# Values weighted by three products of rounded halves, and ranks copied out of PSUM by ScalarE

## The reference

```python
# attention over each sequence, on an input that the gate has scaled
scores = einsum('bqd,bkd->bqk', Q, K) * scale          # causal
attn = softmax(scores)
out = einsum('bqk,bkd->bqd', attn, V) @ Wo.T            # V @ Wo.T is one product V' here
x = x + out
# a layer per sequence (base layer plus a product of rank 8), applied to x
# then attention over the 32 sequences at each position, with 16 heads and 4 key-value heads,
# a router, and two of 8 experts for each of the 8192 rows (a dropped row beyond each expert's capacity)
```

## Time and profile before

| | |
|---|---|
| Three runs | 1309.61, 1312.0, 1320.82 us; median 1312.0 |
| Profiled execution | 1307.97 us, its span 1306.1 us |
| Mean granted TensorE clock | 0.93 of full speed |
| Busy over the span: TensorE, VectorE, ScalarE, GpSimd | 88%, 68%, 64%, 44% |
| TensorE busy, sequences 90 to 400 us | 310.0 of 310 us |
| TensorE busy, positions 429 to 765 us | 307.3 of 336 us |

### The profile page before, as it was taken

One profiled execution on the slowest core, in us unless ns is written; L12 is line 12 of the kernel. 1 busy time (PEld: TensorE's weight loads), 2 busy tenths in 40 slices (PEclk: granted clock), 3 DMA queues, 4 the chain that ended last, 5 costly groups with the idle time before them and its releaser, 6 DMA issues. The chain is left out here.

```text
span 1306.1 us, 25180 instructions
## 1 busy us (share of the span) xinstructions
PE 1151.2 (88%) x8121; PEld 1040.6 (80%) x8153; DVE 886.7 (68%) x2214; ACT 831.1 (64%) x1910; POOL 578.6 (44%) x564
## 2 busy tenths in 40 slices
PE   4499999999998898898989874489999999999985
PEld 2289999999997787787778763489989988888975
DVE  2546565656564787887887853697777778787763
ACT  1057666666665697877787652456677766676762
POOL 0012121212121243877787777246655544554455
PEclk9789999999999798988898886699999999999998
DMA  9633232333231122433343447258777768686763
GB/s 314 166 95 120 92 112 92 112 92 112 92 97 49 38 80 71 139 114 121 121 127 120 124 123 229 76 137 190 176 180 183 202 163 198 167 188 177 188 144 49
DMA packets 119517, 175.43 MB, mean 134 GB/s; under 512 B 14880, under 2 KB 89920, under 8 KB 118848
## 3 DMA queue, kind: packets, MB, share of 16 engines
q1 hardware_dynamic: 92800, 139.63, 34.7%
q0 software_dynamic: 26592, 34.24, 14.0%
HBM read 107.96 MB, written 67.69 MB: 134 GB/s over the span
## 5 line engine op out<-in xcount | busy, mean ns | idle before, releaser
L1548 POOL DMA_INDIRECT out_rows<-y,row x142 | 237.3, 1671 | 238.8 <-DVE y L1777 120.8
L1651 ACT ACTIVATE hh<-ph 128x512 fp32r<-128x512 f32 (+1 forms) x172 | 95.1, 553 | 154.4 <-issue 128.1
L1708 DVE TENSOR_TENSOR hl<-h,hh 128x512 fp32r<-128x512 f32 (+1 forms) x172 | 102.7, 600 | 94.3 <-ACT h L1652 80.4
L175 PE MATMUL py<-w2h,hh 128*128 128x256 f32 x568 | 160.7, 283 | 1.7 <-DVE y L1777 1.1
L177 PE MATMUL py<-w2h,hl 128*128 128x256 f32 x568 | 160.7, 283 | 0.0
L176 PE MATMUL py<-w2l,hh 128*128 128x256 f32 x568 | 160.7, 283 | 0.0
L175 PE MATMUL ph<-xh,w1h 128*128 128x512 f32 (+1 forms) x344 | 128.9, 375 | 34.2 <-issue 27.8
L1113 POOL DMA_INDIRECT slot_rows<-kept,slot x112 | 116.0, 1036 | 32.8 <-issue 30.8
L176 PE MATMUL ph<-xl,w1h 128*128 128x512 f32 (+1 forms) x344 | 125.4, 364 | 0.0
L177 PE MATMUL ph<-xh,w1l 128*128 128x512 f32 (+1 forms) x344 | 124.8, 363 | 0.0
L175 PEld LDWEIGHTS py<-w2h,hh 128*128 128x128 f32 x568 | 108.9, 192 | 2.9 <-issue 1.9
(11 more groups left out here) (309 smaller groups left out, 3565.0 us busy)
## 6 DMA issues: line engine op xcount, KB each, us to landing
w1e<-in_moe_w SPq DMA_DIRECT2D x43, 512.0 KB
w2e<-in_moe_w SPq DMA_DIRECT2D x43, 512.0 KB
x_rows<-x SPq DMA_DIRECT2D x64, 256.0 KB, 2.3
xg<-x_rows SPq DMA_DIRECT2D x64, 256.0 KB
xr<-slot_rows SPq DMA_DIRECT2D x28, 532.0 KB
xT<-in_xT SPq DMA_DIRECT2D x32, 256.0 KB, 2.8
x<-in_x SPq DMA_DIRECT2D x32, 256.0 KB, 3.5
out_rows<-res SPq DMA_DIRECT2D x64, 128.0 KB
```

The lines of the kernel that those rows point to most:

```text
L175: nc.tensor.matmul(out, at_a(ah), at_b(bh), start=first, stop=False, skip_group_check=True)
L1548: g.indirect_dma_start(out=out, out_offset=bass.IndirectOffsetOnAxis(ap=row[m % NR][:, t:t + 1], axis=0), in_=y[m % 2][:, t, :], in_offset ...
L1651: a.activation(hh[m % 2][:, f, 0:n], ph[f][:, 0:n], ACT.Gelu_apprx_tanh)
L1708: v.tensor_tensor(hl[m % 2][:, f, 0:n], h[:, f, 0:n], hh[m % 2][:, f, 0:n].bitcast(F32), ALU.subtract).then_inc(hl_did, 1)
```

## The change

In the sequences stage pT and vv become pairs of fp32r tiles. ScalarE writes the high parts, VectorE the low ones: the rest of v behind the reciprocals, the rest of pT behind u and ahead of kv. The six fp32 products become 18 of `three`. vv has no memory of its own any more and lies in that of qT, and ScalarE's copy of v waits for the y of the step before.

In the positions stage the rank products move ahead of the logits products, and wait for h1 and for the logits copy of step k - 4 instead of the copy of k - 3. ScalarE copies the ranks (64 columns, and the counts of the early batch with them) to an SBUF tile right behind the first logits copy. VectorE's `place` reads this tile, and TensorE's wait is on ScalarE's copy (`rank_out`).

```diff
--- before.py
+++ after.py
@@ -632,9 +632,9 @@
         qT = parts("qT", [P, DC, T])
-        vv = bufs("vv", [P, TC, D])
+        vv = qT
         pz = bufs("pz", [P, T + P])
-        pT = bufs("pT", [P, T + P])
+        pT = [tuple(sb(f"pT{u}_{part}", [P, T + P], F32R) for part in ("high", "low")) for u in places]
         x12 = bufs("x12_", [P, TC, 2, D])
@@ -651,7 +651,7 @@
         pe_did = {n: sem(f"pe_{n}_") for n in "layer qT nT x1T score v kv q pT x2 y".split()}
-        dve_did = {n: sem(f"dve_{n}_") for n in "x1 layer qT nT x1T max rden u kv st mv shift".split()}
+        dve_did = {n: sem(f"dve_{n}_") for n in "x1 layer qT nT x1T max rden u kv st mv shift v pT".split()}
         act_did = {n: sem(f"act_{n}_") for n in "layer qT nT x1T exp v uh q pT x2 nrm".split()}
@@ -727,7 +727,7 @@
                         after(pe, dve_did["u"], k, u)
-                        after(pe, act_did["v"], k - 1, u)
+                        after(pe, dve_did["v"], k - 1, u)
                         for mc in range(DC):
@@ -787,12 +787,12 @@
                     for u in places:
-                        after(pe, act_did["pT"], k, u)
-                        after(pe, act_did["v"], k, u)
-                        t.matmul(pa[u][:, 0:D], pT[u][:, 0:P], vv[u][:, 0, :], start=True, stop=True)
+                        after(pe, dve_did["pT"], k, u)
+                        after(pe, dve_did["v"], k, u)
+                        three(nc, pa[u][:, 0:D], pT[u], vv[u], lambda a: a[:, 0:P], lambda b: b[:, 0, :], True, True)
                         for c in range(TC):
-                            ins = t.matmul(pa[u][:, D:2 * D], pT[u][:, (c + 1) * P:(c + 2) * P], vv[u][:, c, :],
-                                           start=(c == 0), stop=(c == TC - 1))
+                            ins = three(nc, pa[u][:, D:2 * D], pT[u], vv[u], lambda a: a[:, (c + 1) * P:(c + 2) * P],
+                                        lambda b: b[:, c, :], c == 0, c == TC - 1)
                         ins.then_inc(pe_did["y"], 1)
@@ -829,7 +829,8 @@
                         after(act, pe_did["v"], k, u)
-                        a.copy(flat(vv[u]), pb[u][:]).then_inc(act_did["v"], 1)
+                        after(act, pe_did["y"], k - 1, u)
+                        a.copy(flat(vv[u][0]), pb[u][:]).then_inc(act_did["v"], 1)
                 if has(k + 1):
@@ -850,7 +851,7 @@
                         after(act, pe_did["pT"], k, u)
-                        a.copy(pT[u][:], pa[u][:, 0:T + P]).then_inc(act_did["pT"], 1)
+                        a.copy(pT[u][0][:], pa[u][:, 0:T + P]).then_inc(act_did["pT"], 1)
                 if has(k - 1):
@@ -935,6 +936,10 @@
                         v.reciprocal(rden[:, u, :], den[:, u, :]).then_inc(dve_did["rden"], 1)
+                if has(k):
+                    for u in places:
+                        after(dve, act_did["v"], k, u)
+                        rest(flat(vv[u][1]), pb[u][:], flat(vv[u][0])).then_inc(dve_did["v"], 1)
                 if has(k + 1):
@@ -943,6 +948,10 @@
                         ins.then_inc(dve_did["u"], 1)
+                if has(k):
+                    for u in places:
+                        after(dve, act_did["pT"], k, u)
+                        rest(pT[u][1][:], pa[u][:, 0:T + P], pT[u][0][:]).then_inc(dve_did["pT"], 1)
                 if has(k - 2):
@@ -1019,10 +1028,11 @@
         early = table_work(sb, EARLY)
-        early_counts = sb("early_counts", [P, E])
+        ranks = sb("ranks", [P, BATCH * E + E])
         routing = sem("routing")
         ratio_in, ratio_did = sem("ratio_in"), sem("ratio_did")
-        chosen_did, ranked, rank_free = sem("chosen_did"), sem("ranked"), sem("rank_free")
+        chosen_did, ranked, rank_out = sem("chosen_did"), sem("ranked"), sem("rank_out")
+        placed = sem("placed")
         routed, counted = sem("routed"), sem("counted")
@@ -1143,7 +1153,7 @@
                 for m in chosen_at(k - 2):
-                    pe.wait_ge(rank_free, m + 1)
+                    pe.wait_ge(rank_out, m + 1)
                 if has(k - 2):
@@ -1178,6 +1188,23 @@
                         ins.then_inc(pe_did["av"], 1)
+                for m in chosen_at(k - 1):
+                    first, n = BATCHES[m]
+                    out = rank[:, 0:2 * n * E].rearrange("p (b e) -> p b e", e=E)
+                    pe.wait_ge(chosen_did, m + 1)
+                    after(pe, dve_did["h1"], min(k - 2, I2 - 1), 0)
+                    after(pe, act_did["logit"], min(k - 4, I2 - 1), 0)
+                    t_.matmul(out, pr.strictb[:], pr.chosen[:, 2 * first:2 * (first + n), :],
+                              start=True, stop=False, skip_group_check=True)
+                    ins = t_.matmul(out, pr.onesb[:], before[:, :, 0:2 * n].rearrange("p e b -> p b e"),
+                                    start=False, stop=True, skip_group_check=True)
+                    if m == EARLY_BATCH:
+                        ins = t_.matmul(ps_h[0][:, COUNTED:COUNTED + E], pr.onesb[:], before[:, :, 2 * n],
+                                        start=True, stop=True, skip_group_check=True)
+                    ins.then_inc(ranked, 1)
+                    if m == len(BATCHES) - 1:
+                        t_.matmul(ps_s[1][:, 0:E], pr.onesb[:], before[:, :, 2 * n], start=True, stop=True
+                                  ).then_inc(counted, 1)
                 if has(k - 3):
@@ -1186,21 +1213,6 @@
                         ins.then_inc(pe_did["logit"], 1)
-                for m in chosen_at(k - 1):
-                    first, n = BATCHES[m]
-                    out = rank[:, 0:2 * n * E].rearrange("p (b e) -> p b e", e=E)
-                    pe.wait_ge(chosen_did, m + 1)
-                    after(pe, act_did["logit"], min(k - 3, I2 - 1), 0)
-                    t_.matmul(out, pr.strictb[:], pr.chosen[:, 2 * first:2 * (first + n), :],
-                              start=True, stop=False, skip_group_check=True)
-                    t_.matmul(out, pr.onesb[:], before[:, :, 0:2 * n].rearrange("p e b -> p b e"),
-                              start=False, stop=True, skip_group_check=True).then_inc(ranked, 1)
-                    if m == EARLY_BATCH:
-                        t_.matmul(ps_h[0][:, COUNTED:COUNTED + E], pr.onesb[:], before[:, :, 2 * n],
-                                  start=True, stop=True, skip_group_check=True).then_inc(counted, 1)
-                    if m == len(BATCHES) - 1:
-                        t_.matmul(ps_s[1][:, 0:E], pr.onesb[:], before[:, :, 2 * n], start=True, stop=True
-                                  ).then_inc(counted, 1)
@@ -1208,6 +1220,14 @@
             a.activation(warm[:], pr.cst[:, 0:1], ACT.Exp)
+
+            def take_ranks(m):
+
+                act.wait_ge(ranked, m + 1)
+                if m > 0:
+                    act.wait_ge(placed, m)
+                n = BATCH * E + (E if m == EARLY_BATCH else 0)
+                a.copy(ranks[:, 0:n], ps_h[0][:, D + P:D + P + n]).then_inc(rank_out, 1)
@@ -1264,6 +1284,12 @@
                         a.copy(pr.logits[:, group(k - 3, u), :], ps_h[u][:, D:D + E]).then_inc(act_did["logit"], 1)
+                        if u == 0:
+                            for m in chosen_at(k - 1):
+                                take_ranks(m)
+                else:
+                    for m in chosen_at(k - 1):
+                        take_ranks(m)
                 if has(k - 2):
@@ -1340,14 +1366,13 @@
                 start = pr.cst[:, C_BASE:C_BASE + E].unsqueeze(1).broadcast_to([P, B, E])
-                dve.wait_ge(ranked, m + 1)
-                if m == EARLY_BATCH:
-                    dve.wait_ge(counted, 1)
-                    rt.step(v.tensor_copy(early_counts[:], ps_h[0][:, COUNTED:COUNTED + E]))
-                ins = v.tensor_tensor(S1[:, 0:B], rank[:, 0:B * E].rearrange("p (b e) -> p b e", e=E), start, ALU.add)
-                ins.then_inc(rank_free, 1)
+                dve.wait_ge(rank_out, m + 1)
+                rt.step(v.tensor_tensor(S1[:, 0:B], ranks[:, 0:B * E].rearrange("p (b e) -> p b e", e=E), start,
+                                        ALU.add))
                 yield
-                dve.wait_ge(rank_free, m + 1)
+                rt.wait()
+                if m != EARLY_BATCH:
+                    dve.sem_inc(placed, 1)
                 for k in range(K):
@@ -1376,7 +1401,8 @@
                 if m == EARLY_BATCH:
-                    yield from early_table(nc, pr, rt, early, early_counts[:])
+                    yield from early_table(nc, pr, rt, early, ranks[:, BATCH * E:BATCH * E + E])
+                    dve.sem_inc(placed, 1)
                     dve.sem_inc(pr.planned, 1)
@@ -1445,7 +1471,7 @@
             pipeline(dve, step)
-            dve.wait_ge(counted, 2)
+            dve.wait_ge(counted, 1)
             rt.link(v.tensor_copy(pr.counts[:], ps_s[1][:, 0:E]))
...
```

## The result

The changed kernel takes 1348.5 us (median of 4 runs, 1337.8 to 1356.7), the kernel before 1311.6 on the same chip: ratio 1.0265, interval 1.0176 to 1.0354. It is slower, as forecast, and by 36.9 us where 23 were forecast. The profiled execution is the longest of the four (1356.7 us), so differences between the two profiles add up to more than the medians' 36.9.

A forecast was written before the change was run, and what follows sets the result against it. TensorE's order of work was taken to bound the sequences stage, waits and a slow clock part of the positions stage. Sequences +51.0 and ranks -28.4 gave +22.6 on 1307.97: 1331 us, range 1304 to 1350.

The forecast's parts named there:

- the case forecast: Whole kernel: stalls at x2 and low clock outweigh the ranks' gain; 1331 us, own range 1320 to 1342, chance 0.60.
- The rival in which the positions stage gives back what the ranks free: Positions stage: TensorE later waits for VectorE's choosing and the clock falls there; gain only -10 to -14, 1347 us, chance 0.10.
- Products times values: Sequences stage, TensorE: 18 products of halves replace six fp32 ones; -0.52 us a step, -8.3 us over 16 steps.
- Rest of the values: Sequences stage, VectorE: two added subtractions a step fit into its idle time before uT_high; 0.
- Rest of the probabilities: Sequences stage: pT rests ahead of kv on VectorE make TensorE's x2 wait 2.8 us, 14 times; +39.6 us.
- Clock: Sequences stage: 11 of 14 stalls bring a half-clock stretch costing 1.7 us each; +18.7 us.
- The rival that the clock stays up: Sequences stage: stalls cost 2.8 us and no more, without a clock fall; 1312 us, chance 0.20.
- First steps: Start of the sequences stage: the first step has no x2 to cover the pT rests; about +1 us.
- Ranks: Positions stage: rank products no longer wait for the logits copy, and scores run at full clock; -28.4 us.
- the second rival of the prediction: Positions stage: it gives back what the ranks free, through waits for VectorE's choosing and low clock; 1347 us, chance 0.10.
- Experts: Experts stage, from 765 us on: not touched by the change; 0.

The follow-up runs named there:

- e3: The changed kernel with only VectorE's rest of pT moved behind its copy of kv; ratio 0.9895 to the kernel before, 1261.2 us.
- e6: The changed kernel run again, unaltered, beside the kernel before on another chip; ratio 1.0329.
- e4: The changed kernel with 20 unread 128x256 products put on TensorE between the transposes and x2; ratio 1.0223 to the kernel before, 1301.9 us.
- e1: The sequences part of the change alone, with the positions stage of the kernel before; ratio 1.0446, 1331.9 against 1273.9 us.
- e7: The kernel before with only the rank products moved ahead of the logits, VectorE reading ranks from PSUM, no ScalarE copy; ratio 0.9889.
- e5: The kernel before run again, unaltered, for a second profile; ratio 0.9988.
- e2: The positions part of the change alone, with the sequences stage of the kernel before; ratio 0.9915, 1262.6 us.
- e10: The sequences part with VectorE's rest of pT behind kv, and the positions stage of the kernel before; ratio 1.000.

## Why the prediction was right, and where its sizes were off

The sum, 1331, was 17.5 us below the median of 1348.5; the case forecast, a stop at x2 and a low clock behind it, is the one that came. 1348.5 is inside the range of 1304 to 1350, by 1.5 us, and outside the 1320 to 1342 of the forecast case. Between the profiles the forecast is 26 us short, 6.4 in the sequences, 7.8 in the positions and 11.9 in the experts, all to one side. The rival in which the positions stage gives back what the ranks free named 1347, nearer than the forecast; that is luck, since most of those batches kept their gain (below). By its steps:

- **Products times values, -8.3.** Right in kind. Without the stop a step is 21.33 us (e3) where it was 21.74: -0.41, over 16 steps -6.6. Forecast was -0.52 a step. From the last start of x2's products to L724 it went from 2.80 to 2.37 us, of which the products with the values are 2.68 and 2.25. The spacing of 0.12 us held from the first product to the last, and not the 0.109 of the formula that the prediction quotes; there is a weight load for each of these products. What the sum left out is the end of the group, 0.21 us to the next product. The last of the 18 in e3, and the next:

```profile
251.39 0.28 PE L177 MATMUL pa<-qT_high,pT_low 128*128 128x256 f32 x1
251.60 0.61 PE L724 MATMUL pc<-stack 24*128 24x256 f32 x3
```

- **Rest of the values, 0.** Right: no wait on it in the steady steps, in after or in e3.
- **Rest of the probabilities, 14 x 2.8 = 39.6.** Right, in place, cause, count and size. Measured 3.38 - 0.57 = 2.81 us later, times 14, 39.3. The rest that had no row, 128x384, was put at 0.55 us halfway between its neighbours and took 0.553:

```profile
L899 DVE TENSOR_TENSOR pT_low<-pa,pT_high 128x384 fp32r<-128x384 f32 x28 | 14.3, 553 | 33.9 <-ACT pT_high L854 33.9
```

- **Clock, 11 x 1.7 = 18.7.** Right in kind; it came 14 times at 25.62 - 24.14 = 1.48 us, 20.7 in all (24.14 is e6's step with a stop and no low stretch, the same as 21.33 + 2.81; e4's filled one was 24.21). The 1.7 was half of the stretch, as if products took twice as long in it. They don't:

```profile
274.51 0.28 PE L177 MATMUL pd<-layer_high,x1T_low 128*128 128x256 f32 x1
...
275.46 0.28 PE L176 MATMUL pd<-layer_low,x1T_high 128*128 128x256 f32 x1
...
276.16 0.41 PE L177 MATMUL pd<-layer_high,x1T_low 128*128 128x256 f32 x1
```

  Eight spacings from 274.51 to 275.46 are 0.119 us each, ten from 276.16 to 278.29 (above) 0.213, 1.8 times as much. Some 16 products fall into a stretch of 3.4 us, and 16 x 0.094 is 1.5. The rival that the clock stays up fell. The Trainium skill (TensorE: Matmul & The Clock Gate, Why this matters for your kernels) warns only of gaps above about 3 us; here 2.56 us were enough in 40 of 42 stops (after, e1, e6).
- **First steps, +1.** Mis-sized: 57.4 less (39.3 + 20.7 - 6.6) leaves +4.0. Of this 1.8 us are no part of the step: the first probabilities' transposes come at 76.5 us in place of 74.7, and over all profiles this start lies between 73.4 and 76.5. The first step is 0.8 longer than 17.69 - 0.41: its first values product waits 3.0 us for the pT rest, where it waited 2.0 for pT before. The second step, 22.61 us, is 1.3 longer than 21.33, and was not in the sum; 0.6 of it is a wait for the rest of qT, and where the others come from stays open.
- **Ranks, -28.4.** The mechanism was right (no wait, full clock, e7), the size not: -20.6 in the first pair of profiles and -11.7 between e6 and e5. The second is smaller because the stage of before was 12.4 us shorter in e5 (354.8) than in the profile the forecast was made on (367.2, the longest of five). The first is taken apart here. Batch by batch: the four intervals of a batch were forecast at 9.05 (rank), 9.2 (place), 9.6 and 11.3 (choose). In batches 3 to 5 they were 9.21, 9.97, 9.88 and 10.93, together 40.0 for the 44.27 of the earlier trace rows; the batch shown above has 9.83, 9.07, 9.98 and 10.94. Four batches gave -17.8 for the -20.5 forecast, the first -4.8 for -4.4, and the two steps ahead of all ranks -1.3. What failed most is the end: the sixth batch, which runs into the early table, was to give -2.5 and cost +2.0, the tail was to give -1 and cost +1.2. VectorE, then TensorE of the kernel after, and TensorE of before at the same point:

```profile
778.42 0.69 DVE L1423 TENSOR_REDUCE gmax<-gs 128x16 f32<-128x512 f32 x1 [0.24 <-DVE table L254]
...
790.89 0.69 DVE L1423 TENSOR_REDUCE gmax<-gs 128x16 f32<-128x512 f32 x1 [5.03 <-PE gs L1143]
```

```profile
781.53 1.11 PE L1180 MATMUL gv<-cst,kept 128*128 128x128 f32 x4 [4.45 <-ACT vb L1258]
```

```profile
749.62 0.70 PE L1170 MATMUL gv<-cst,kept 128*128 128x128 f32 x4 [0.41 <-issue]
```

  The step with the table is filled by VectorE and takes 14.77 us in both. TensorE, now earlier done with its part, waits 4.45 us for ScalarE behind it, where it waited 0.41 before; the clock is low from about 781 to 798, VectorE waits 5.03 us for scores made at it, and the next step takes 12.47 us where it took 8.81. In e2, e3 and e4 that step took 12.47 us too, in e6 10.31 and in e7 9.80, so the size of this loss differs from run to run. It is the second rival of the prediction in small, at one place. In the batches before it that rival's mechanism isn't there, as the clock is 0.99 (third window of the kernel after).
- **Experts, 0.** They are the same code, and took +11.9 us in the first pair of profiles. GpSimd's waits in that stage, first before, then after:

```profile
POOL out_rows L1548 <- DMA out_rows<-y,row: 72.7, 20, 6.6
```

```profile
POOL out_rows L1574 <- DMA out_rows<-y,row: 152.3, 34, 7.0
```

  Its scatters end more of its waits in this execution. The sum of its waits grew by less than these rows say, as those for VectorE's y fell from 120.8 to 54.8 us: together 193.5 before and 207.1 after. Between e5 and e6 the stage differs by 3.2 us (485.7, 488.9), and the waits for scatters are alike (70.9 and 70.0). The same sign, 34 waits of 159.0 us, stands in e1's long execution, whose other runs were 18 to 22 us shorter. So this comes and goes with the execution, and nothing points to the change. It may be what sets the two longer runs of the changed kernel (1356.2, 1356.7) off from the two shorter ones (1337.8, 1340.8), but the shorter ones have no profile.

What stays open: why the experts' scatters differ, what the second step of the sequences waits for, and why e6's ratio of 1.0329 is above the first pair's 1.0265; their intervals overlap by 0.009, so it may be nothing.

## What to carry to other kernels

An instruction that waits should be last on its engine among those whose inputs are ready: the same small subtractions cost 4% in front of kv (e1) and nothing behind it (e10). Price an added wait by what is queued behind it, through to the bounding engine, then add the clock: the low clock behind a stop of 2.81 us cost half as much again here (1.48 us). When a part moves and a part is copied, test the two alone; here the move was the whole gain.

## What the hardware did that was not expected

**Two close lengths of waiting.** In the sequences stage half clock followed 40 of 42 stops of 2.56 us, 3 of 14 of 2.10 us, and none where the gap was filled with 20 products. No row of before shows that half a microsecond changes so much. The length is not all that decides: two of the 42 weren't followed, and in the less dense positions stage of before 1.32 us were the earlier trace rows. What else does is not shown.

**Small copies of VectorE beside GpSimd.** The positions stage of the same kernel took 354.8 and 367.2 us in two profiles, before any change. One difference stands in single instructions. The copy of 128x64 bf16 after a choosing, on VectorE, first before, then after (min/median/max ns):

```profile
L1327 DVE COPY taken<-chosen x8: 304/1095/1100, 499.0 to 791.9; 128x64 bf16<-128x64 bf16 x8
```

```profile
L1353 DVE COPY taken<-chosen x8: 297/303/311, 554.9 to 827.9; 128x64 bf16<-128x64 bf16 x8
```

One slow one, with what GpSimd does at that time:

```profile
542.23 1.09 DVE L1327 COPY taken<-chosen 128x64 bf16<-128x64 bf16 x1
```

```profile
542.12 2.05 POOL L1105 TENSOR_TENSOR pw<-pw,gden 128x512 f32<-128x512 f32 x2
```

It takes 0.30 us, or 1.10 when it starts inside GpSimd's multiplication of the weights. Above it starts 0.11 us behind GpSimd and ends at 543.33, 0.17 us behind the end of GpSimd's first multiplication (543.16). This holds for every slow one. Over all 13 profiles 21 of 104 copies were slow; each began 0.11 or 0.12 us inside a GpSimd instruction on whole tiles and ended 0.17 or 0.18 us behind it. Beside GpSimd's shorter addition (0.7 us) that gives 0.78, as here in before:

```profile
719.10 0.78 DVE L1327 COPY taken<-chosen 128x64 bf16<-128x64 bf16 x1
```

The scan behind the copy takes 0.31 us alone, 0.60 beside the addition and up to 0.97 beside the multiplication, and then also ends 0.16 or 0.17 us behind GpSimd. Kernels with the ranks last have two to six slow copies, those with the ranks moved at most one (none in after). The Trainium skill (SBUF — State Buffer, Who interferes with whom) says that these two engines share one pair of ports, that copies on VectorE can take it, that an instruction with two inputs in SBUF contends for it with a GpSimd instruction that reads SBUF, and that the later one is blocked. The rows agree with it, but no run here changed this alone, so the ports as its cause are not shown. It can explain a part of why the choosing step came to 10.93 us in place of 11.3, and, with the low clock (96.7 us in one profile of before, 77.2 in the other), of why that stage took 367.2 and 354.8 us.
